# Cross-attention scores of a Perceiver block: high queries against high and low contexts in one 512-column product, the halves added together with the row maximum

## The chip, the core and the metric

One core of a Trainium2 chip runs the whole program. The metric is device time in microseconds (us) of one execution. The core has five engines that run their own in-order instruction lists and meet at semaphores: TensorE (PE; its weight loads are listed as PEld), VectorE (DVE), ScalarE (ACT), GpSimd (POOL) and SyncE (SP, which issues the transfers). Products land in PSUM, which has eight banks of 512 fp32 columns; everything else lies in SBUF.

## The reference, cut to what matters

```python
x = x + xattn(layernorm(x), ctx_768)     # the stage that is changed
x = x + attn(layernorm(x))               # relative-position attention
x = x + ffn(layernorm(x))                # fake-quantised gated FFN

# xattn: x (64, 32, 512), ctx (64, 257, 384), 16 heads of 64
q = (hidden_states @ Wq).reshape(B, S, H, Dh).transpose(0, 2, 1, 3)
k = (encoder_hidden_states @ Wk)...      # likewise
v = (encoder_hidden_states @ Wv)...
scores = jnp.einsum('bhsd,bhkd->bhsk', q, k) * scale
probs = jax.nn.softmax(scores, axis=-1)  # over the 257 context rows
out = jnp.einsum('bhsk,bhkd->bhsd', probs, v)
out = out.transpose(0, 2, 1, 3).reshape(B, S, H * Dh) @ Wo + bo
```

## The kernel before

The cross attention never forms the keys. A first stage multiplies each head's queries with that head's key weights, so that a query becomes a row of 384 numbers (`qk`) to be multiplied with the context itself. The last context row is subtracted from the other 256, which leaves the softmax as it is and makes the score of the last row zero.

To keep fp32 accuracy on a faster product, operands are held as two parts, a rounded high part and the low remainder; a product is the sum of three: high x high, high x low, low x high (`PARTS`).

Work goes by tiles of 128 tokens, 16 of them (`t`), each of four batches of 32 tokens (`b`). Tile 0 is the section "first", tile 1 "second", tiles 2 to 14 run in a loop, tile 15 is "last". In a batch, 16 heads x 32 queries make 512 score rows, in four row groups of 128 (`rg`). For one batch and row group, here called a unit, `pe_scores` (L656) multiplies `qk` (stationary, 128x128) with the transposed context `cT` (moving): three chunks of the 384 numbers, three products each, into one PSUM bank. The four units use the banks s0, s1, q0 and q1. VectorE takes the negated row maximum (`row_max`, L1200), ScalarE the exponential with its row sum straight out of PSUM (`exp`, L899), which frees the bank; VectorE inverts the sum, and ScalarE (units 0 and 1) or VectorE (units 2 and 3, `norm`) scales the row.

The written order of each engine fixes what stands behind what. TensorE's in one batch is: scores of unit 0; transposes of the probabilities of the batch before (`pe_probsT`, banks t0 and t1); scores of units 1 and 2; in the second batch the value-weight products of the heads of the tile before (`pe_wv`); scores of unit 3; first value product (`pe_pv`, banks o0 and o1 in turn, so the third one needs the bank of the first); two of three transposes of the next context (`pe_ctxT`, banks t0, t1 and t0 again, so the third one needs the bank of the first); second value product; in the fourth batch the output projection (`pe_wo`, in bank q1, the bank of unit 3's scores) with the third transpose in its middle, otherwise the third transpose; third value product.

Each transposed bank is copied by ScalarE as the high part (`act_high`, L779) and then subtracted by VectorE as the low part (`dve_low`, L976), which frees the bank. VectorE adds the last context row's share to each value product (`dve_attended`, L1182). In the fourth batch ScalarE and VectorE also split the next tile's `qk` into its parts (`act_qk_high`, `dve_qk_low`). GpSimd subtracts the last row from the contexts and splits them.

The columns for the last context row: `cT` has 258 columns, of which two are zero. In the first tile all products run over 258 columns and leave the zero score in the bank; later only the unit in bank q1 after an output projection does, the other banks keep the zero.

## Time and profile before

| | |
|---|---|
| median of 3 runs | 1561.62 us (1560.56 to 1562.24) |
| the profiled execution, its own time | 1560.53 us |
| its span, first to last instruction | 1558.7 us |
| mean granted TensorE clock | 0.997 |
| busy: TensorE, its weight loads, VectorE, ScalarE, GpSimd | 1525.8, 1281.1, 1048.9, 737.6, 381.5 us |

The span is what the views below divide; the profiled execution's own time is 1.8 us more, for what lies around it. A line such as L669 is a line of the kernel. Products are pipelined, so the duration shown for one (some 0.28 us for 256 columns) is longer than the time after which the next one starts; cadences are read from groups of many. Where a group of products waits, its weight load (PEld) waits ahead of it.

### The profile page before, as it was taken

How to read it: one execution, taken by the hardware profiler on the slowest of the kernel's cores; microseconds unless marked ns; L12 is line 12 of the kernel's file. 1: busy time of each engine (PE TensorE's matmuls, PEld its weight loads, DVE VectorE, ACT ScalarE, POOL GpSimd, SP SyncE). 2: the span in 40 equal slices, each digit the busy share in tenths (PEclk: the TensorE clock that was granted, in tenths of full speed). 3: DMA queues.
4: the chain of work that ended last, by engine and by line, in shares of the span. 5: the costliest groups of instructions: out<-in, count | busy, mean ns of one | idle time of the engine just before them, and what ended most of it. 6: DMA issues, size and time to landing. Idle time of an engine off the chain costs nothing.

```text
span 1558.7 us, 35878 instructions
## 1 busy us (share of the span) xinstructions
PE 1525.8 (98%) x13706; PEld 1281.1 (82%) x13714; DVE 1048.9 (67%) x2255; ACT 737.6 (47%) x1601; POOL 381.5 (24%) x228
## 2 busy tenths in 40 slices
PE   7999989999999999999999999999999999998989
PEld 5888788999999899989989898888888888886544
DVE  7666677677667766676677767647555654556788
ACT  5445655455545554555455554443222232234755
POOL 1000444343444344444434353500000000000000
PEclk9999999999999999999999999999999999999999
DMA  6899773341434133422343144250220311325022
GB/s 229 321 365 374 304 271 137 132 153 47 140 136 143 61 124 140 140 87 98 140 140 122 63 140 140 82 203 21 83 97 29 116 49 43 116 54 151 1 107 108
DMA packets 90270, 210.72 MB, mean 135 GB/s; under 512 B 17025, under 2 KB 45889, under 8 KB 87361
## 3 DMA queue, kind: packets, MB, share of 16 engines
q1 hardware_dynamic: 90176, 209.39, 37.7%
q8 instruction: 70, 1.15, 0.3%
q14 instruction: 24, 0.19, 0.0%
HBM read 137.54 MB, written 68.94 MB: 132 GB/s over the span
## 4 chain that ended last, share of the span: by engine, by line
PE 90%; issue 6%; DVE 3%; ACT 1%; DMA 0%; SPq 0%; POOLq 0%; POOL 0%
PE psum_o L693 17%; PE psum_s L669 9%; PE psum_q L669 8%; PE psum_o L1518 6%; PE psum_q L1562 6%; PE psum_q L723 6%; PE psum_q L1518 6%; PE psum_t L1594 6%; PE psum_o L557 6%; PE psum_o L708 5%; PE psum_t L681 3%; PE psum_t L638 3%; PE psum_t L589 1%; PE psum_q L589 1%; PE psum_s L1549 1%
## 5 line engine op out<-in xcount | busy, mean ns | idle before, releaser
L693 PE MATMUL psum_o<-pT,c_nat 128*128 128x512 f32 x1152 | 307.4, 403 | 3.4 <-issue 2.4
L693 PEld LDWEIGHTS psum_o<-pT,c_nat 128*128 128x128 f32 x1152 | 204.5, 189 | 40.2 <-DVE pT L980 3.6
L1332 POOL TENSOR_TENSOR c_nat<-c_raw,constants 128x768 fp32r<-128x768 f32 x64 | 93.8, 1466 | 551.4 <-PE psum_o L693 441.7
L1187 DVE TENSOR_SCALAR oT<-psum_o,c_last 128x512 f32<-128x512 f32 x192 | 143.4, 747 | 66.4 <-PE psum_o L693 66.3
L902 ACT ACTIVATE probs<-psum_s,nmax 128x257 f32<-128x257 f32 x128 | 61.1, 477 | 233.8 <-DVE nmax L1202 233.8
L669 PE MATMUL psum_s<-cT,qk 128*128 128x256 f32 (+1 forms) x1152 | 163.6, 286 | 1.3 <-DVE cT L980 1.2
L669 PEld LDWEIGHTS psum_s<-cT,qk 128*128 128x128 f32 x1152 | 150.0, 189 | 7.4 <-DVE cT L980 1.4
L669 PE MATMUL psum_q<-cT,qk 128*128 128x256 f32 (+1 forms) x1152 | 151.8, 283 | 0.3 <-DVE qk L1119 0.3
L669 PEld LDWEIGHTS psum_q<-cT,qk 128*128 128x128 f32 x1152 | 142.2, 189 | 3.1 <-issue 2.6
L980 DVE TENSOR_TENSOR pT<-psum_t,pT 128x512 fp32r<-128x512 f32 x128 | 87.6, 686 | 71.0 <-ACT pT L781 71.0
L1317 POOL TENSOR_TENSOR c_raw<-c_raw,last_row 128x768 f32<-128x768 f32 x64 | 120.2, 1878 | 24.2 <-DMA last_row<-in_ctx_dram 19.4
L1335 POOL TENSOR_TENSOR c_nat<-c_raw,c_nat 128x768 fp32r<-128x768 f32 x64 | 118.1, 1846 | 5.0
L2334 POOL PARTITION_ALL_REDUCE tiny<-tiny x1 | 0.4, 381 | 424.9 <-DVE tiny L2250 424.9
L781 ACT ACTIVATE cT<-psum_t 128x256 fp32r<-128x256 f32 x192 | 67.3, 388 | 76.4 <-PE psum_t L638 76.2
L1119 DVE TENSOR_TENSOR qk<-raw,qk 128x1536 fp32r<-128x1536 f32 x59 | 103.0, 1748 | 0.0
L833 ACT ACTIVATE qk<-raw 128x1536 fp32r<-128x1536 f32 x64 | 94.7, 1515 | 0.0
L708 PE MATMUL psum_o<-oT,wv 128*64 128x128 f32 x1536 | 87.4, 274 | 0.2 <-issue 0.2
L557 PE MATMUL psum_o<-xnT,wq 128*128 128x512 f32 x372 | 87.1, 392 | 0.0
L708 PEld LDWEIGHTS psum_o<-oT,wv 128*64 128x64 f32 x1536 | 83.5, 137 | 2.4 <-issue 0.4
L1562 PE MATMUL psum_q<-w2v_high,xnT 128*128 128x512 f32 x256 | 84.5, 396 | 0.0
L557 PEld LDWEIGHTS psum_o<-xnT,wq 128*128 128x128 f32 x372 | 69.2, 188 | 16.9 <-issue 2.1
L1518 PE MATMUL psum_o<-xnT,w2k_high 128*128 128x512 f32 x256 | 80.5, 395 | 0.0
(292 smaller groups left out, 3098.9 us busy)
## 6 DMA issues: line engine op xcount, KB each, us to landing
qk_by_tile<-staged SPq DMA_DIRECT2D x32, 1536.0 KB, 10.2
raw<-qk_by_tile SPq DMA_DIRECT2D x16, 3072.0 KB, 12.5
c_raw<-in_ctx_dram SPq DMA_DIRECT2D x64, 384.0 KB, 3.2
last_row<-in_ctx_dram SPq DMA_DIRECT2D x64, 192.0 KB, 4.3
out_dram<-x_out SPq DMA_DIRECT2D x32, 256.0 KB, 2.0
x_res<-in_x_dram SPq DMA_DIRECT2D x16, 256.0 KB, 2.7
x_in<-out_dram SPq DMA_DIRECT2D x4, 1024.0 KB, 7.7
x_all<-out_dram SPq DMA_DIRECT2D x1, 4096.0 KB, 13.4
```

Source lines behind the costliest of these rows:

```text
L557: m = pe.matmul(ps[:], wq[:, j, part, k, :], xnT[:, moving, k, :, :], start=(k, part, moving) == (0, 0, 0), stop=(k, part) == (KD - 1, 1))
L669: m = pe.matmul(ps[:, 0:keys], qk[:, rg, part, c, b, :], cT[b % 2][:, moving, c, 0:keys], start=(c, part, moving) == (0, 0, 0), stop=(c, p ...
L693: i = pe.matmul(ps[:], c_nat[(b - 1) % 2][:, part, k, m * P:(m + 1) * P], pT[:, moving, k, :], start=(k, part, moving) == (0, 0, 0), stop= ...
L708: i = pe.matmul(ps[64 * par:64 * par + 64, h4 * P:(h4 + 1) * P], wv[:, c, head * DH:(head + 1) * DH], oT[:, c, slot, :, :], start=c == 0, ...
L833: nc.scalar.activation(qk[:, rg, 0, :, :, :].rearrange("p c b (h q) -> p h (c b) q", h=4), raw[:, :, rg, :].rearrange("p h (a q) -> p h a ...
L1119: nc.vector.tensor_tensor(part[1], raw[:, :, rg, :].rearrange("p h (a q) -> p h a q", q=SQ), part[0].bitcast(F32), ALU.subtract).then_inc( ...
L1187: nc.vector.tensor_scalar(oT[:, m, :, (b - 1) % 4, :], ps[:].rearrange("p (s q) -> p s q", q=SQ), c_last[:, (b - 1) % 2, m:m + 1], None, A ...
L1317: nc.gpsimd.tensor_tensor(c_raw[i][:], c_raw[i][:], row_, ALU.subtract).then_inc(s_sub, 1)
L1332: G.tensor_tensor(flat(c_nat[i][:, 0, :, :]), flat(c_raw[i][:]), zero.to_broadcast([P, 2 * DC]), ALU.add).then_inc(s_chi, 1)
L1335: G.tensor_tensor(c_nat[i][:, 1, :, :], c_raw[i][:], c_nat[i][:, 0, :, :].bitcast(F32), ALU.subtract).then_inc(s_nat, 1)
L1518: m = pe.matmul(ps[:], (w2_high[w], w2_low[w])[part][:, k, j * P:(j + 1) * P], xnT2[:, moving, k, :, :], start=(k, part, moving) == (0, 0, ...
L1562: m = pe.matmul(ps[:], xnT2[:, part, k, i, :], w[moving][:, k, 512 * n:512 * (n + 1)], start=(k, part, moving) == (0, 0, 0), stop=(k, part ...
```

## The change

The two products with the high queries (against the high and the low context) become one of 512 columns, whose halves land side by side in the bank; the product of the low queries adds to the first half. So a unit is six products instead of nine, and its scores are the sum of two halves. ScalarE copies the second half from PSUM to the probability tile; VectorE adds the first half to it, writes the negated sum there and takes the running minimum of it, from 0.0 on for the last row's zero score, in one instruction; ScalarE's exponential then reads the probability tile in place. A semaphore step stands ahead of VectorE's instruction. Nothing puts the last row's zero score into the bank any more: GpSimd zeroes that column of the probability tile for each batch. The fills of `cT`'s zero columns go. ScalarE's order is rewritten: the four copies (`half`) are put in, and unit 0's exponential moves between the two probability copies.

```diff
@@ -655,19 +659,16 @@
 
         def pe_scores(pe, t, b, rg, section):
 
-            if section == "first" and rg == 0 and b < 2:
-                pe.wait_ge(s_zero, b + 1)
             if b == 0:
                 pe.wait_ge(s_qlo, 4 * t + (rg + 1))
             ps, done = empty(pe, U1(("S", b, rg), t, section))
 
-            keys = SKP if section == "first" or (b, rg) == (0, 3) else 2 * P
+            keys = 2 * P
             for c in range(KC):
                 if rg == 0:
                     wait_chunk(pe, t, b, section, c)
-                for part, moving in PARTS:
-                    m = pe.matmul(ps[:, 0:keys], qk[:, rg, part, c, b, :], cT[b % 2][:, moving, c, 0:keys],
-                                  start=(c, part, moving) == (0, 0, 0), stop=(c, part) == (KC - 1, 1))
+                m = pe.matmul(ps[:], qk[:, rg, 0, c, b, :], cT[b % 2][:, :, c, 0:keys], start=c == 0, stop=False)
+                m = pe.matmul(ps[:, 0:keys], qk[:, rg, 1, c, b, :], cT[b % 2][:, 0, c, 0:keys], start=False, stop=c == KC - 1)
             m.then_inc(done, 1)
 
         def pe_probsT(pe, t, b, section):
@@ -896,11 +897,19 @@
         def act_cross_tile(act, t, section):
             begun, more = section != "first", section != "last"
 
+            def half(b, rg):
+                ps, _ = full(act, U1(("S", b, rg), t, section))
+                nc.scalar.activation(probs[b % 2][:, rg, 0:2 * P], ps[:, 2 * P:4 * P], ACT.Copy).then_inc(s_half, 1)
+
             def exp(b, rg):
-                bk, _ = U1(("S", b, rg), t, section)
+                if rg == 0 and section == "first" and b < 2:
+                    act.wait_ge(s_zero, 2)
+                elif rg == 0:
+                    act.wait_ge(s_blank, 4 * t + (b - 1))
                 act.wait_ge(s_max, 16 * t + (4 * b + rg + 1))
-                nc.scalar.activation(probs[b % 2][:, rg, 0:SK], bank[bk][:, 0:SK], ACT.Exp, bias=nmax[:, rg:rg + 1],
-                                     accum_out=den[:, rg:rg + 1]).then_inc(drained[bk], 1)
+                both = probs[b % 2][:, rg, 0:SK]
+                nc.scalar.activation(both, both, ACT.Exp, bias=nmax[:, rg:rg + 1], scale=-1.0,
+                                     accum_out=den[:, rg:rg + 1]).then_inc(drained[U1(("S", b, rg), t, section)[0]], 1)
 
             def scale(b, rg):
                 act.wait_ge(s_rden, 16 * t + (4 * b + rg + 1))
@@ -911,30 +920,38 @@
                 act_high(act, U1(("CT", b, c), t, section), cT[(b + 1) % 2][:, 0, c, 0:2 * P], cols(2 * P))
 
             if not begun:
+                half(0, 0)
+                half(0, 1)
                 exp(0, 0)
                 exp(0, 1)
                 ctxT(0, 0)
                 ctxT(0, 1)
                 scale(0, 0)
                 ctxT(0, 2)
+                half(0, 2)
                 exp(0, 2)
                 scale(0, 1)
                 scale(0, 2)
+                half(0, 3)
                 exp(0, 3)
                 scale(0, 3)
                 act_last_scalars(act, t, 0, section)
             for b in range(0 if begun else 1, 4):
                 after = more or b < 3
-                exp(b, 0)
+                half(b, 0)
                 if late_turn(b, section):
-                    exp(b, 1)
+                    half(b, 1)
                 for k in range(2):
                     act_probsT(act, t, b, k, section)
+                    if k == 0:
+                        exp(b, 0)
+                if not late_turn(b, section):
+                    half(b, 1)
                 if b == 3 and more:
                     act_qk_high(act, t + 1, 0)
-                if not late_turn(b, section):
-                    exp(b, 1)
+                exp(b, 1)
                 scale(b, 0)
+                half(b, 2)
                 exp(b, 2)
                 scale(b, 1)
                 if b == 1 and section == "second":
@@ -945,6 +962,7 @@
                         act_wv(act, t, n, section)
                 if b == 1 and section == "second":
                     act_wo_high(act, 3)
+                half(b, 3)
                 exp(b, 3)
                 if b == 3 and more:
                     act_qk_high(act, t + 1, 1)
@@ -1155,7 +1173,6 @@
                 else:
                     for c in range(2):
                         dve_start_context(dve, c)
-                    nc.vector.memset(cT[0][:, :, :, 2 * P:SKP].bitcast(F32), 0.0).then_inc(s_zero, 1)
                 for j in range(4, 8):
                     dve_group_qk(dve, s, j)
                     if (s, j) == (GROUPS - 1, 4):
@@ -1198,8 +1215,12 @@
             begun, more = section != "first", section != "last"
 
             def row_max(b, rg):
-                ps, _ = full(dve, U1(("S", b, rg), t, section))
-                nc.vector.tensor_reduce(nmax[:, rg:rg + 1], ps[:, 0:SK], AX_X, ALU.max, negate=True).then_inc(s_max, 1)
+                bk, _ = U1(("S", b, rg), t, section)
+                dve.wait_ge(s_half, 16 * t + (4 * b + rg + 1))
+                dve.sem_inc(s_halfseen, 1)
+                both = probs[b % 2][:, rg, 0:2 * P]
+                nc.vector.tensor_tensor_reduce(both, bank[bk][:, 0:2 * P], both, -1.0, 0.0, ALU.add, ALU.min,
+                                               nmax[:, rg:rg + 1]).then_inc(s_max, 1)
 
             def inverse(b, rg):
                 taken(dve, U1(("S", b, rg), t, section))
@@ -1215,7 +1236,9 @@
                 dve_cross_low(dve, ("CT", b, c), t, section, v[:, 1, c, 0:2 * P], v[:, 0, c, 0:2 * P], 2 * P)
 
             if not begun:
-                nc.vector.memset(cT[1][:, :, :, 2 * P:SKP].bitcast(F32), 0.0).then_inc(s_zero, 1)
+                full(dve, U1(("S", 0, 0), t, section))
+                for i in range(2):
+                    nc.vector.memset(probs[i][:, :, 2 * P:SK], 0.0).then_inc(s_zero, 1)
                 row_max(0, 0)
                 row_max(0, 1)
                 inverse(0, 0)
@@ -1341,6 +1364,15 @@
             pool.wait_ge(s_xres, 16 * t)
             nc.gpsimd.tensor_tensor(x_res[:], x_res[:], bo_all[:], ALU.add).then_inc(s_xb, 1)
 
+        def pool_blank(pool, t, b, section):
+
+            if b:
+                taken(pool, U1(("S", b - 1, 3), t, section))
+            else:
+                pool.wait_ge(drained["q1"], U1.before("q1", t, section, 1))
+            pool.sem_inc(s_blankseen, 1)
+            nc.gpsimd.memset(probs[(b - 1) % 2][:, :, 2 * P:SK], 0.0).then_inc(s_blank, 1)
+
         def pool_qk_low(pool, t, rg):
 
             pool.wait_ge(s_qhi, 4 * t + (rg + 1))
@@ -1356,9 +1388,11 @@
             for rg in range(4):
                 pool_qk_low(pool, 0, rg)
             pool_split(pool, 0, 1, "first")
+            pool_blank(pool, 0, 1, "first")
             for b in range(2, 4):
                 pool_less_last(pool, 0, b)
                 pool_split(pool, 0, b, "first")
+                pool_blank(pool, 0, b, "first")
             pool_less_last(pool, 0, 4)
             full(pool, U1(("S", 3, 1), 0, "first"))
             pool.wait_ge(s_qlo, 4 + 1)
@@ -1370,10 +1404,12 @@
                     pool.wait_ge(s_qlo, 4 * t + 4)
                     pool_less_last(pool, t, b + 1)
                     pool_split(pool, t, b, section)
+                    pool_blank(pool, t, b, section)
                     continue
                 pool_split(pool, t, b, section)
                 if section != "last" or b < 3:
                     pool_less_last(pool, t, b + 1)
+                pool_blank(pool, t, b, section)
                 if b == 1:
                     pool_bias(pool, t)
             if section == "last":
```

The hunk left out declares the four semaphores `s_half`, `s_halfseen`, `s_blank` and `s_blankseen`.

## Rows read from the trace of the kernel before

**Rows 1.** The page: busy time of TensorE, share of the span, instructions.

```profile
PE 1525.8 (98%) x13706; PEld 1281.1 (82%) x13714; DVE 1048.9 (67%) x2255; ACT 737.6 (47%) x1601; POOL 381.5 (24%) x228
```

**Rows 2.** One tile by batches: stretch, length, busy of each engine, clock, DMA share, GB/s.

```profile
588.54:598.46 9.92, 9.92 (x69) 9.05 (x68) 7.47 (x20) 5.06 (x16) 5.11 (x3) 1.00 0.60 184
598.46:614.11 15.65, 15.65 (x167) 14.44 (x165) 8.05 (x20) 6.38 (x18) 6.32 (x4) 1.00 0.47 193
614.11:624.11 10.00, 10.00 (x69) 9.10 (x68) 6.74 (x18) 5.07 (x16) 5.11 (x3) 1.00 0.20 59
624.11:639.59 15.48, 15.48 (x94) 13.60 (x92) 13.27 (x22) 10.18 (x20) 5.12 (x3) 1.00 0.12 38
```

**Rows 3.** Chain of waits, same tile: start, length, what, number of instructions.

```profile
602.81 5.39 PE psum_o L708 x96
...
617.30 2.12 PE psum_q L669 x18
...
632.63 2.74 PE psum_q L723 x12
```

**Rows 4.** Timeline, third batch, TensorE and weight loads: start, length, what.

```profile
614.11 1.24 PE L669 MATMUL psum_s<-cT,qk 128*128 128x256 f32 x9
...
619.14 1.24 PEld L693 LDWEIGHTS psum_o<-pT,c_nat 128*128 128x128 f32 x6
...
622.26 0.37 PEld L638 LDWEIGHTS psum_t<-ident,c_raw 128*128 128x128 f32 x2
```

**Rows 5.** Timeline, third batch, ScalarE; in brackets idle time and its releaser.

```profile
616.32 1.08 ACT L781 ACTIVATE pT<-psum_t 128x512 fp32r<-128x512 f32 x2
618.00 0.48 ACT L902 ACTIVATE probs<-psum_s,nmax 128x257 f32<-128x257 f32 x1 [0.60 <-DVE nmax L1202]
...
619.93 0.46 ACT L902 ACTIVATE probs<-psum_q,nmax 128x257 f32<-128x257 f32 x1
620.29 0.19 ACT L902 ACTIVATION_READ_ACCUMULATOR probs<-psum_q,nmax 128x1 f32 x1
621.07 0.66 ACT L781 ACTIVATE cT<-psum_t 128x256 fp32r<-128x256 f32 x2 [0.59 <-PE psum_t L638]
```

**Rows 6.** Timeline, third batch, VectorE.

```profile
617.55 0.41 DVE L1202 TENSOR_REDUCE nmax<-psum_s 128x1 f32<-128x257 f32 x1
617.88 0.68 DVE L980 TENSOR_TENSOR pT<-psum_t,pT 128x512 fp32r<-128x512 f32 x1
618.48 0.15 DVE L1206 RECIPROCAL rden<-den 128x1 f32<-128x1 f32 x1
...
621.66 0.73 DVE L980 TENSOR_TENSOR cT<-psum_t,cT 128x256 fp32r<-128x256 f32 x2
```

**Rows 7.** Groups by line and shape: busy us, mean ns of one, idle before, releasers.

```profile
L1119 DVE TENSOR_TENSOR qk<-raw,qk 128x1536 fp32r<-128x1536 f32 x59 | 103.0, 1748 | 0.0
L833 ACT ACTIVATE qk<-raw 128x1536 fp32r<-128x1536 f32 x64 | 94.7, 1515 | 0.0
...
L980 DVE TENSOR_TENSOR cT<-psum_t,cT 128x256 fp32r<-128x256 f32 x192 | 73.8, 412 | 2.0 <-ACT cT L781 1.9
...
L781 ACT ACTIVATE cT<-psum_t 128x256 fp32r<-128x256 f32 x192 | 67.3, 388 | 76.4 <-PE psum_t L638 76.2
...
L907 ACT ACTIVATE probs<-probs,rden 128x256 f32<-128x256 f32 x130 | 66.1, 509 | 6.0 <-DVE rden L1206 1.2
...
L902 ACT ACTIVATE probs<-psum_s,nmax 128x257 f32<-128x257 f32 x128 | 61.1, 477 | 233.8 <-DVE nmax L1202 233.8
...
L1202 DVE TENSOR_REDUCE nmax<-psum_s 128x1 f32<-128x257 f32 x128 | 53.5, 418 | 16.8 <-PE psum_s L669 16.8
```

**Rows 8.** Timeline, fourth batch: first output-projection load, third context transpose's load.

```profile
632.24 0.19 PEld L723 LDWEIGHTS psum_q<-wo_high,aT_high 128*128 128x128 f32 x1
...
634.98 0.37 PEld L638 LDWEIGHTS psum_t<-ident,c_raw 128*128 128x128 f32 x2
```

**Rows 9.** Timeline, third batch, GpSimd's last instruction.

```profile
617.78 1.84 POOL L1317 TENSOR_TENSOR c_raw<-c_raw,last_row 128x768 f32<-128x768 f32 x1
```

More of the change, by code:

```diff
@@ L448, in build_kernel @@
         s_zero = sem("last_scores_zeroed")
+        s_half = sem("second_scores_copied")
+        s_halfseen = sem("second_scores_seen")
+        s_blank = sem("last_score_blanked")
+        s_blankseen = sem("exponentials_seen")
         s_chi = sem("ctx_high_ready")
```

## The prediction, made before the changed kernel ran

> **What bounds the kernel now.** I read four views, in this order. The page says that TensorE is busy for 98% of the span [rows 1]. The table by stretches, cut at the starts of the four batches of one token tile in the middle of the loop, says what a tile costs: 9.92, 15.65, 10.00 and 15.48 us, 51.05 in all. TensorE is busy in every microsecond of it at a granted clock of 1.00, while ScalarE works 51%, 41%, 51% and 66% of the time [rows 2]. So here a nanosecond taken from TensorE is a nanosecond gained, as long as nothing makes it wait. The chain of waits gives the cadences of its products: 18 of 256 columns in 2.12 us are 118 ns each, 12 of 512 columns in 2.74 us are 228 ns each [rows 3]. The timeline of the third batch, last, gives the order in which ScalarE and VectorE serve TensorE, and how long before its use each thing is ready [rows 4 to 6].
>
> **What the change takes from TensorE.** A unit (one batch, one of four row groups) has nine products of 256 columns now, 9 x 0.118 = 1.06 us. After, it has three of 512 and three of 256, 3 x (0.228 + 0.118) = 1.04 us. The number of columns stays; only three instructions' fixed part goes. That is about 0.025 us a unit, 0.10 a batch, 6 to 7 us over 256 units. If the 256-column products now wait for their weight loads (loads of 128 columns end up about as dense as the products), one behind a 512 could cost as little as 0.228 - 0.118 = 0.110: then 13 us. These are the ends of the gain; I take 0.10 a batch. The Trainium skill (TensorE: Matmul & The Clock Gate, "Back-to-back issue gap") has the gap as N/2.4 + 2.5 ns, which is 109 and 216 ns; the rows are 118 and 228, and a unit would gain 7 ns by the page, 2 us in all. Row and page differ, and I go by the row.
>
> **What it adds.** Per unit: ScalarE copies 256 columns from PSUM, 0.39 us by the same copy of the context transposes [rows 7]. VectorE's maximum (0.42 [rows 7]) gives way to one instruction that adds a PSUM and an SBUF operand, writes the sum and keeps a running minimum. No row shows it. Below it cannot be cheaper than an addition of the same shape, 0.41 [rows 7]; above it could cost the two passes that it fuses, 0.41 + 0.33 (a reduction that starts behind another instruction, from its start to the next start [rows 6]) = 0.75. It is nearest to an addition, and ScalarE's form with a sum read afterwards ends 0.09 later than the exponential alone (619.93 to 620.48 against 0.46 [rows 5]), so I take 0.41 + 0.09 = 0.50. VectorE also gets a separate semaphore step ahead of each: between nothing and 0.07, what a one-element reciprocal adds to the queue (0.15, of which 0.08 lie under the instruction ahead: 617.88 + 0.68 against 618.48 [rows 6]); I take 0.05. Exponentials read SBUF: 0.51 as the scaling does, against 0.48 [rows 7]. A hand-over between engines is 0.04 (maximum done 617.55 + 0.41 = 617.96, exponential at 618.00 [rows 5, 6]). An engine takes its next instruction some 0.1 before the last one ends (620.29 against 619.93 + 0.46 [rows 5]).
>
> The cost is not the busy time, of which both engines have room, but the order. For each unit ScalarE copies, VectorE fuses, ScalarE takes the exponential, and each queue is served in order. Behind an exponential that waits for the minimum stand ScalarE's scaling of earlier rows, the next unit's copy and, in the end, the context copies. I walk through the third batch with the trace's times of before.
>
> - Unit 0: product done 615.32 (614.11 + 1.24 = 615.35 now [rows 4]), copied 615.36 to 615.75, fused 615.84 to 616.34. The first probability copy now goes ahead of the exponential (615.80), exponential 616.38, second copy 616.88 to 617.47. It ended at 616.32 + 1.08 = 617.40 before [rows 5]. Nothing lost.
> - Unit 1: its copy stands behind that, 617.37 to 617.75; fused 617.85 to 618.35. The second probability low part on VectorE follows, 618.26 to 618.96, 0.4 later than before (617.88 + 0.68 [rows 6]). The first value product's weights load at 619.14 now [rows 4] and want to at 619.05: covered, with 0.05 left.
> - Exponential 1 at 618.38; inverse behind the low part, 618.88; scaling 619.07; copy 2 619.48 to 619.87; fused 619.96 to 620.46; exponential 620.50; scaling 621.00; copy 3 621.40 to 621.79; fused 621.88 to 622.38; exponential 3 at 622.42 with its sum read by 623.01. Before it stood at 619.93 [rows 5]: 2.5 us late.
> - Late next: the context copies on ScalarE, 622.92 (621.07 before [rows 5]), and VectorE's low part of the first, 623.35 to 623.76 (started 621.66 before [rows 6]). The third context transpose uses that bank; its weights load at 622.26 [rows 4] and would at 622.16. It can't before 623.80. TensorE stands for 1.64 us.
> - The third value product waits for VectorE's addition on its bank, done at 623.12: behind the stall, covered. The next batch's first scores too.
>
> Net of the 0.10 saved: +1.55 us. The first batch of a tile has the same order: +1.65 by the same walk. The second has 5.39 us of head products between the third and the fourth unit [rows 3], so the chain of three is over before the fourth starts: it only gains, -0.1. In the fourth batch a query copy (1.51 [rows 7]) stands between copy 1 and exponential 1, so by the same steps from 624.11 exponential 3 starts at 632.93 and its sum is read at 633.52. The output projection uses that unit's bank and loaded its first weights at 632.24 [rows 8]: it could at 632.14 and must wait until 633.56, 1.4 us. Then ScalarE's second query copy ends at 634.94; VectorE has one query low part (1.75 [rows 7]) and an addition ahead of the next, which runs from 635.28, and ends the context low part at 637.36; and the third transpose, due 634.98 - 0.10 + 1.42 = 636.30 [rows 8], waits another 1.1. Net +2.4.
>
> A tile: 1.65 - 0.1 + 1.55 + 2.4 = 5.5. Fourteen tiles are whole: 77. The first has no head or output products but the same chains in three batches, about 5; the last has no transposes in its last batch, about 4. Sum 86 us on 1560.5 of the profiled execution, which is 1.1 below the median of the runs: **1648**.
>
> Costed at nothing: GpSimd's zeroing of the last column. It stands behind a subtraction that ends at 617.78 + 1.84 = 619.62 [rows 9], and its reader is the exponential of the following batch, some 6 us later; were it not covered, every batch's first exponential would be late by what it lacks. Removed zero fills and 258-column products are too few to count.
>
> **Bounds.** Four fused instructions lie in series in the first and third batch (unit 0's by way of the second probability copy), two or three in the fourth. With 0.41 and no semaphore step: 4 x 0.14 = 0.56 less in each, 0.3 in the fourth, 4.1 a tile, 57 + 7 on 1560.5: 1625. With 0.75 and 0.07: 4 x 0.27 = 1.08 more in each and 0.8 in the fourth, 8.5 a tile, 119 + 13 on 1560.5: 1693.
>
> **The rivals.**
> - *The fused instruction costs nearly two passes*: 0.65 to 0.83. For it: two input streams, a written stream and a running value in one instruction, of which no row has a like. Against: two-input additions from PSUM run at the pace of one-input reductions (0.41 and 0.42 [rows 7]). Ten lie in series in a tile, so in 15.5 tiles each 0.1 is 15.5 us: 1671 to 1699, chance 0.22. The Trainium skill (Vector Engine (DVE) Microarchitecture Reference, "Points that are easy to get wrong") says that the shape with accumulator halves its throughput when both sources are non-bf16 in SBUF. Here one is in PSUM, so by its words it should not; no run here shows it.
> - *TensorE stays the bound*, on the other side: the chains end in time, and only the fewer instructions show: 1547 to 1555. It decides at one place: the first context low part must end by 622.12, 0.05 us after it does now. For it, ScalarE is idle half of the time. Against, 234 us of that idle time are already waits of exponentials for the row maximum [rows 7], and a queue in order adds to them. Chance 0.05.
> - *The saved and the lost cancel*, because copies overlap more than I allow: chance 0.02. Slower, but by less than 1618: 0.04.
>
> **How the numbers follow.** My forecast has 0.67, 1618 to 1670 by itself. The range 1618 to 1702 takes in the walk's bounds and the first rival; outside lie the other 0.11 and some 0.05 above. What a measurement of this kernel tells from no change is about 0.2%, 3 us. Faster 0.05, within 0.02, slower 0.93.
>
> **What would show it.** In the new trace: 118 and 228 ns in mixed order; fused instructions of about 0.5; TensorE idle ahead of the third context transpose in three batches of four, put down to VectorE's context low part, and ahead of the output projection, put down to an exponential; ScalarE waiting some 0.7 us for the minimum ahead of three exponentials of each batch; batches of 11.5, 15.6, 11.5 and 17.9 us. I would be wrong if the fused instruction ran far from 0.5, if the semaphore steps cost much more, or if TensorE, idle 1.6 us at a time, were granted a lower clock than its full stretches show [rows 2].

## The result, and the profile after

The changed kernel takes 1649.83 us (median of 4 runs, 1649.05 to 1652.97), against 1561.76 for the kernel before in the same session: a ratio of 1.0569, 95% interval 1.0551 to 1.0587. The profiled execution has a span of 1647.9 us, 89.2 more than before. Predicted were 1648, with a range of 1618 to 1702.

The page of the changed kernel, busy time and the shares of its chain of waits, answers to [rows 1]:

```profile
PE 1541.8 (94%) x12946; PEld 1238.9 (75%) x12946; DVE 1062.1 (64%) x2511; ACT 836.2 (51%) x1857; POOL 388.0 (24%) x291
...
PE 57%; issue 16%; DVE 14%; ACT 11%; DVEq 1%; ACTq 0%; DMA 0%; SPq 0%; POOLq 0%; POOL 0%
```

The shares of the chain of the kernel before:

```profile
PE 90%; issue 6%; DVE 3%; ACT 1%; DMA 0%; SPq 0%; POOLq 0%; POOL 0%
```

VectorE is hardly busier than before and ScalarE is at half of the span. No engine became the bound by its load; TensorE fell from 98% to 94%, and VectorE and ScalarE now hold a quarter of the chain instead of 4%. The share of "issue" rose too: in the cross stage it lies in the short gaps between the steps of VectorE and ScalarE. One tile by batches (first the third batch, then the fourth, first and second) answers to [rows 2]:

```profile
601.67:613.05 11.38, 10.14 (x57) 8.42 (x56) 6.91 (x22) 6.62 (x20) 5.18 (x4) 1.00 0.16 52
613.05:630.69 17.64, 15.89 (x81) 12.83 (x80) 12.95 (x27) 11.78 (x24) 5.18 (x4) 1.00 0.10 33
630.69:642.15 11.46, 10.25 (x57) 8.38 (x56) 8.04 (x24) 6.62 (x20) 5.41 (x4) 1.00 0.68 215
642.15:657.63 15.48, 15.48 (x153) 13.71 (x152) 8.48 (x25) 7.89 (x22) 6.39 (x5) 1.00 0.39 154
```

Three of four batches have a hole in TensorE's time, at a clock of 1.00; the second has none. The tile is 55.96 instead of 51.05. To compare single batches, one border in [rows 2] has to be moved: the second batch is taken there from 598.46, but its first product starts 0.10 later:

```profile
598.56 1.23 PE L669 MATMUL psum_s<-cT,qk 128*128 128x256 f32 x9
```

From that start, the first two batches of before are 10.02 and 15.55 us, not 9.92 and 15.65, and the second one became 0.07 us shorter.

The timeline of the next third batch, which begins at 657.63, is the chain itself. It stands against [rows 4 to 6] with 43.52 us taken off:

```profile
661.47 0.43 DVE L1222 CUSTOM_DVE_ANT_0 probs<-psum_s,probs 128x256 f32<-128x256 f32 x1 [0.82 <-ACT probs L902]
661.82 0.08 DVE L1222 DVE_READ_ACCUMULATOR2_ANT nmax<- 128x1 f32 x1
...
661.94 0.52 ACT L911 ACTIVATE probs<-probs,nmax 128x257 f32<-128x257 f32 x1 [0.65 <-DVE nmax L1222]
...
664.95 0.36 ACT L902 ACTIVATE probs<-psum_q 128x256 f32<-128x256 f32 x1
...
665.50 0.42 DVE L1222 CUSTOM_DVE_ANT_0 probs<-psum_q,probs 128x256 f32<-128x256 f32 x1 [1.41 <-ACT probs L902]
...
665.96 0.51 ACT L911 ACTIVATE probs<-probs,nmax 128x257 f32<-128x257 f32 x1 [0.65 <-DVE nmax L1222]
...
666.47 0.64 ACT L782 ACTIVATE cT<-psum_t 128x256 fp32r<-128x256 f32 x2
666.87 0.76 DVE L998 TENSOR_TENSOR cT<-psum_t,cT 128x256 fp32r<-128x256 f32 x2
...
667.35 0.20 PEld L642 LDWEIGHTS psum_t<-ident,c_raw 128*128 128x128 f32 x2 [1.68 <-DVE cT L998]
667.35 0.44 PE L642 MATMUL psum_t<-ident,c_raw 128*128 128x128 f32 x2 [1.24 <-DVE cT L998]
```

The same product before:

```profile
622.49 0.38 PE L638 MATMUL psum_t<-ident,c_raw 128*128 128x128 f32 x2
```

Read the chain from the bottom. TensorE's weight load waited 1.68 us for VectorE's context low part; that waited for ScalarE's context copy; that stood in ScalarE's queue behind exponential 3, and exponential 3 waited 0.65 us for the minimum, whose fused instruction had to wait for the copy. The walk had these ends at 622.42 (exponential 3), 622.92, 623.35 and 623.80; the trace, shifted, has 622.44, 622.95, 623.35 and 623.83. Only the starts of the fused instructions are some 0.10 late (665.50 is 621.98, the walk: 621.88).

The fourth batch of the tile, to be set against [rows 8] with 11.06 us added:

```profile
622.47 0.50 PE L724 MATMUL psum_q<-wo_high,aT_high 128*128 128x512 f32 x1 [0.93 <-ACT probs L911]
...
626.29 0.44 PE L642 MATMUL psum_t<-ident,c_raw 128*128 128x128 f32 x2 [0.82 <-DVE cT L998]
```

The output projection starts at 633.53 in the time of before (the walk: 633.56), the third transpose at 637.35 (the walk: about 637.4). Groups by line and shape give the new instruction:

```profile
L1222 DVE CUSTOM_DVE_ANT_0 probs<-psum_q,probs 128x256 f32<-128x256 f32 x128 | 54.4, 425 | 146.1 <-ACT probs L902 146.1
...
L1222 DVE DVE_READ_ACCUMULATOR2_ANT nmax<- 128x1 f32 x256 | 21.4, 84 | 0.0
```

Fused instruction and read-out of the minimum together end 0.43 us after the start (661.47 to 661.82 + 0.08 = 661.90 in the timeline above), not 0.50.

**Where the 89.2 us lie.** From the starts of the probability transposes: 1.9 ahead of the first, 5.3 in the first tile, 6.8 in the second, 4.92 in each of the 13 after, 2.7 in the last, 80.8 in all (the last one starts at 996.65 before and 1077.42 after). The other 8.4 come *after* the cross stage, where the change edits nothing: from that transpose to the end are 562.1 us before and 570.5 after. The chain of waits at the end of the self-attention stage of the changed kernel, and then the windows around it:

```profile
1483.69 1.08 issue
...
1496.46 3.39 issue
...
1500.74 10.75 PE psum_t L1630 x36
```

```profile
1495.00:1500.00 5.00, 1.61 (x102) 1.15 (x105) 1.73 (x4) 0.00 (x0) 0.00 (x0) 0.89 0.55 220
1500.00:1505.00 5.00, 5.00 (x50) 4.07 (x51) 1.42 (x4) 1.81 (x6) 0.00 (x0) 0.50 0.01 3
```

and the same place before:

```profile
1414.01 8.40 PE psum_t L1594 x36
```

Within the last stretch of small value products (32 columns) TensorE stood for 3.39 us for nothing that the profile names. Then the same 36 products of 512 columns took 10.75 us instead of 8.40: for the first 5 us the granted clock was 0.50, the lower of its two levels (1.2 GHz), and over all 10.75 us it was 0.77 in the mean; ahead of that TensorE had been busy 1.61 us of 5. Stall and slow products are 5.7 of the 8.4 us. Three shorter gaps of the same kind, 0.47, 1.08 and 0.27 us between 1419 and 1490, where the kernel before has none above 0.25, make 1.8 more; some 0.9 was not traced. This part was nobody's prediction, and the experiments had to find it as well.

### The profile page after: what moved, and what is told of

Its sections match the earlier page's. It is cut to its first block, busy times and chain, and to the rows that moved or that the text cites. A ratio compares the mean times of both kernels' runs of the same rounds, so it can differ in the third digit from the quotient of the medians.

```text
span 1647.9 us, 35554 instructions
## 1 busy us (share of the span) xinstructions
PE 1541.8 (94%) x12946; PEld 1238.9 (75%) x12946; DVE 1062.1 (64%) x2511; ACT 836.2 (51%) x1857; POOL 388.0 (24%) x291
## 3 DMA queue, kind: packets, MB, share of 16 engines
q8 instruction: 69, 1.13, 0.3%
## 4 chain that ended last, share of the span: by engine, by line
PE 57%; issue 16%; DVE 14%; ACT 11%; DVEq 1%; ACTq 0%; DMA 0%; SPq 0%; POOLq 0%; POOL 0%
PE psum_o L694 7%; PE psum_o L1554 5%; PE psum_t L1630 5%; PE psum_q L1598 5%; PE psum_q L1554 5%; PE psum_o L561 5%; PE psum_o L709 5%; DVE qk L1137 3%; ACT probs L902 3%; ACT probs L911 3%; PE psum_s L670 3%; ACT probs L916 2%; DVE probs L1222 2%; PE psum_t L642 2%; PE psum_q L670 1%
## 5 line engine op out<-in xcount | busy, mean ns | idle before, releaser
L911 ACT ACTIVATE probs<-probs,nmax 128x257 f32<-128x257 f32 x256 | 130.8, 511 | 120.6 <-DVE nmax L1222 119.1
L1222 DVE CUSTOM_DVE_ANT_0 probs<-psum_q,probs 128x256 f32<-128x256 f32 x128 | 54.4, 425 | 146.1 <-ACT probs L902 146.1
L670 PE MATMUL psum_s<-cT,qk 128*128 128x512 f32 x384 | 146.2, 410 | 0.2 <-DVE staged L1117 0.2
L670 PE MATMUL psum_q<-cT,qk 128*128 128x512 f32 x384 | 140.6, 401 | 0.0
L902 ACT ACTIVATE probs<-psum_s 128x256 f32<-128x256 f32 x128 | 48.3, 378 | 163.0 <-PE psum_s L671 163.0
L642 PE MATMUL psum_t<-ident,c_raw 128*128 128x128 f32 x384 | 65.8, 280 | 54.1 <-DVE cT L998 53.5
L1222 DVE CUSTOM_DVE_ANT_0 probs<-psum_s,probs 128x256 f32<-128x256 f32 x128 | 54.2, 424 | 94.7 <-ACT probs L902 94.7
L642 PEld LDWEIGHTS psum_t<-ident,c_raw 128*128 128x128 f32 x384 | 46.0, 141 | 85.8 <-DVE cT L998 74.4
L671 PE MATMUL psum_s<-cT,qk 128*128 128x256 f32 x384 | 107.9, 281 | 0.0
L671 PE MATMUL psum_q<-cT,qk 128*128 128x256 f32 x384 | 107.8, 281 | 0.0
## 6 DMA issues: line engine op xcount, KB each, us to landing
qk_by_tile<-staged SPq DMA_DIRECT2D x32, 1536.0 KB, 10.3
```

Of the source, the lines that this page charges most:

```text
L642: m = pe.transpose(ps[:, k * P:(k + 1) * P], keys[:, k, c * P:(c + 1) * P], ident[:])
L670: m = pe.matmul(ps[:], qk[:, rg, 0, c, b, :], cT[b % 2][:, :, c, 0:keys], start=c == 0, stop=False)
L671: m = pe.matmul(ps[:, 0:keys], qk[:, rg, 1, c, b, :], cT[b % 2][:, 0, c, 0:keys], start=False, stop=c == KC - 1)
L911: nc.scalar.activation(both, both, ACT.Exp, bias=nmax[:, rg:rg + 1], scale=-1.0, accum_out=den[:, rg:rg + 1]).then_inc(drained[U1(("S", b, ...
L1222: nc.vector.tensor_tensor_reduce(both, bank[bk][:, 0:2 * P], both, -1.0, 0.0, ALU.add, ALU.min, nmax[:, rg:rg + 1]).then_inc(s_max, 1)
```

## The experiments

Columns: the median of the 13 tiles in the loop ("tile"), the start of the last probability transpose ("last") and the time from there to the end ("rest"), of the profiled execution; all in us. Ratios are against the kernel before on the same chip.

| kernel | median (runs) | ratio, 95% | tile | last | rest |
|---|---|---|---|---|---|
| before | 1560.9 to 1562.1 | 1 | 51.05 | 996.65 | 562.1 |
| after | 1649.83 (4) | 1.0569 (1.0551–1.0587) | 55.97 | 1077.42 | 570.5 |
| product_alone | 1562.30 (10) | 1.0006 (0.9996–1.0016) | 50.69 | 990.04 | 570.4 |
| chain_alone | 1646.52 (4) | 1.0546 (1.0528–1.0563) | 56.10 | 1079.77 | 564.6 |
| busy_copy | 1566.42 (6) | 1.0034 (1.0021–1.0046) | 51.03 | 995.92 | 568.7 |
| copies_ahead | 1589.12 (4) | 1.0178 (1.0161–1.0195) | 52.17 | 1017.50 | 570.6 |
| step_twice | 1668.73 (4) | 1.0682 (1.0664–1.0700) | 57.06 | 1096.90 | 570.5 |
| order_rewritten | 1563.16 (10) | 1.0010 (1.0000–1.0019) | 50.69 | 992.04 | 568.4 |
| product_padded | 1566.85 (10) | 1.0029 (1.0019–1.0038) | 50.69 | 1001.24 | 564.6 |
| before_padded | 1578.88 (4) | 1.0105 (1.0088–1.0122) | 51.05 | 1007.52 | 571.2 |
| after_split | 1643.51 (4) | 1.0525 (1.0509–1.0541) | 55.98 | 1079.70 | 563.2 |
| order_split | 1556.40 (6) | 0.9971 (0.9959–0.9983) | 50.69 | 991.46 | 561.9 |
| order_split_start | 1554.87 (5) | 0.9961 (0.9947–0.9974) | 50.69 | 990.01 | 563.1 |
| product_split | 1555.38 (4) | 0.9957 (0.9940–0.9974) | 50.69 | 990.79 | 563.0 |

The theory: four instructions a unit in series, in queues served in order. The rivals: load (copies on ScalarE, fused instructions on VectorE), or the products themselves. The first four kernels take the change apart.

**product_alone: the six products without the chain.**

```diff
-                for part, moving in PARTS:
-                    m = pe.matmul(ps[:, 0:keys], qk[:, rg, part, c, b, :], cT[b % 2][:, moving, c, 0:keys],
...
+                m = pe.matmul(ps[:], qk[:, rg, 0, c, b, :], cT[b % 2][:, :, c, 0:keys], start=c == 0, stop=False)
+                m = pe.matmul(ps[:, 0:keys], qk[:, rg, 1, c, b, :], cT[b % 2][:, 0, c, 0:keys], start=False, stop=c == KC - 1)
```

> The kernel before with the six products of 512 and 256 columns alone: the maximum and the exponential read the first half of the bank as before, so the high x low half of the scores is left out. Theory of the serial chain: TensorE stays the bound and only its instructions count, 0.025 us a unit, 6 to 7 us: about 1555 us, 0.996 of before. Rival, that the wide products themselves cost (their operand in two pieces, the bank written over its full width): above 1570.

The tiles gave 0.36 us each, the cross stage ended 6.6 earlier, and the whole won nothing: the rest was 8.3 longer. The time of 1562.30 is thus neither the theory's nor the rival's. So the products are not the loss, and the late 8 us come with them, chain or no chain.

**chain_alone: nine products, with the chain.**

Against the changed kernel, next to the nine products of before:

```diff
-                nc.scalar.activation(probs[b % 2][:, rg, 0:2 * P], ps[:, 2 * P:4 * P], ACT.Copy).then_inc(s_half, 1)
+                nc.scalar.activation(probs[b % 2][:, rg, 0:2 * P], ps[:, 0:2 * P], ACT.Copy, scale=0.0).then_inc(s_half, 1)
```

> The nine products of before with the new chain: ScalarE copies the first half times zero into the probability tile, VectorE adds, ScalarE takes the exponential from there. The scores stay whole. Theory of the serial chain: the chain sets the time of three batches in four, the products only start it 0.03 us later: 1649 to 1653 us. Rival, that the products cost: nearer to 1562 than to 1650.

The chain alone carries the loss in the tiles, 56.10. The time, 1646.5, is 2.5 us under the expected range: the cross stage ended 2.4 us later than in the changed kernel, but the rest is 564.6 instead of 570.5, without the late stall.

**busy_copy: the copy's load without its place in the chain.**

```diff
...
+                nc.scalar.activation(nowhere[:], twice, ACT.Copy).then_inc(s_half, 1)
...
```

> The six products, the maximum and the exponential from PSUM as before, and ScalarE does a copy of 256 columns at each place where the changed kernel has one, after the same wait for the unit's product, but of a constant and to a place that nobody reads. The high x low half of the scores is left out. Theory of the serial chain: the extra copies cost only what they push in ScalarE's queue, at most 1 us a tile, in the fourth batch: 1555 to 1575. Rival, that it is the load on ScalarE (some 100 us more of it): above 1620.

ScalarE was busy 825.0 us, nearly the 836.2 of the changed kernel, and the tile took 51.03 us instead of 55.97. Of the 5.28 us by which the chain lengthens a tile (55.97 - 50.69), ScalarE's load explains 0.34. VectorE's is not in this kernel; order_rewritten has it.

**copies_ahead: the changed kernel, two copies moved up in ScalarE's order.**

```diff
+                half(b, 2)
                 if b == 3 and more:
                     act_qk_high(act, t + 1, 0)
                 exp(b, 1)
                 scale(b, 0)
-                half(b, 2)
+                if not (b == 1 and begun):
+                    half(b, 3)
                 exp(b, 2)
...
-                half(b, 3)
+                if b == 1 and begun:
+                    half(b, 3)
```

> The changed kernel with ScalarE's order alone rewritten: the copy of unit 2 ahead of exponential 1, that of unit 3 ahead of exponential 2 (in the second batch of a tile unit 3 stays where it is), so that no copy stands behind an exponential that waits for VectorE. Same instructions, same work. Theory of the serial chain: the first and third batch come back to 9.9 us, the fourth to 16.9, a tile to 52.4: 1590 us, 1580 to 1602. Rival, that load or the fused instruction's own cost sets the time: 1640 to 1652.

Same instructions, 61 us less. The next minimum is under way while ScalarE still takes the exponential before.

**step_twice: one more semaphore step in the chain.**

```diff
                 dve.sem_inc(s_halfseen, 1)
+                dve.sem_inc(s_halfseen, 1)
```

> The changed kernel with a second semaphore step ahead of each fused instruction. Theory (each unit's copy, step, fused instruction, exponential run one after the other in ScalarE's order, so all that lengthens the chain is paid up to five times a batch in three of four batches): a step of 0.05 to 0.07 us more adds 0.5 to 0.7 us to a tile, 8 to 11 us in all: 1657 to 1661. Rival (VectorE's or ScalarE's load, or the fused instruction's own length, not the chain): VectorE is busy 64% of the span and the step is no work, so 1650, within 2.

The sign and the place were right, the size not: +18.9 us. A step costs more than the walk had allowed. The timeline of step_twice:

```profile
658.87 0.36 ACT L902 ACTIVATE probs<-psum_q 128x256 f32<-128x256 f32 x1
659.51 0.42 DVE L1223 CUSTOM_DVE_ANT_0 probs<-psum_q,probs 128x256 f32<-128x256 f32 x1 [1.09 <-ACT probs L902]
```

From the copy's end to the fused instruction are 0.28 us, against 0.19 in the changed kernel (664.95 + 0.36 to 665.50 above): 0.09 for one step. A tile grew by 1.09, twelve times that, and it grew where the walk has the chain: from one start of the probability transposes to the next, the first batch by 0.41, the third by 0.37 and the fourth by 0.30, four, four and three steps, and the second by nothing. The changed kernel without any step was not tried.

**order_rewritten: both orders anew.** The lists (h copy, p probability part, e exponential, s and n scalings, m minimum, i inverse, a addition of the last key, c context part, q next query part, l last scalars, x output):

```diff
+        ACT_TURN = {"even": "h0 p0 p1 e0 h1 h2 e1 s0 h3 s1 e2 c0 c1 e3 l0 c2",
+                    "last": "p0 h0 p1 q0 h1 h2 e0 h3 e1 e2 e3 c0 q1 c1 l0 s0 s1 q2 c2 q3"}
+        DVE_TURN = {"even": "m0 p0 p1 m1 i0 m2 i1 m3 a0 c0 c1 i2 i3 n2 a1 n3 c2 a2",
+                    "last": "p0 m0 p1 m1 m2 m3 a0 i0 i1 q0 c0 i2 a1 i3 q1 c1 q2 n2 n3 c2 q3 a2 x0"}
```

> The changed kernel with the same instructions, and both ScalarE's and VectorE's orders of the batches written anew (copies ahead of the exponentials, in the fourth batch the scalings and the later query parts behind them; second batches and the first tile nearly as in copies_ahead). Theory (order alone made the loss): TensorE waits nowhere in the middle tiles, which take 50.7 to 51.2 us (50.69 in product_alone): 1589 less 15 times 1.0 to 1.5, so 1565 to 1575, with the stall of the late stage still in it. Rival (part of the loss is load, 128 x 0.38 us of copies on ScalarE and the fused instruction on VectorE, that no order can hide): the fourth batch stays over 16.5 us and the time over 1582.

The tile is 50.69, that of product_alone to the hundredth: copies, steps and fused instructions all fit under TensorE. The time went 2 us below the expected range: of the 25 us gained on copies_ahead in the cross stage, 4.5 are the first tile's (44.6 against 49.0, and 46.1 before), three times what was allowed for it. The copies that it hides are one a unit, 256, not the 128 of the rival.

**The late stall: product_padded and before_padded.** The page of the changed kernel counts 69 packets of the instruction queue for 1.13 MB, so 16 KB each. One of them begins some 1 us into the stall, in the stretch 1497.4 to 1497.9:

```profile
q8 instruction: 1, 0.02, 11.0%
```

The small value products ahead of the stall and behind it, with the clock as the third number from the right:

```profile
1495.36:1496.46 1.10, 1.10 (x88) 0.99 (x88) 1.00 1.07 432
1499.85:1500.74 0.89, 0.89 (x40) 0.76 (x40) 0.50 0.00 0
```

All seven kernels with this stall have it behind the 87th or 88th of these 128 products, and a packet begins 0.8 to 1.3 us after TensorE stopped. So it goes with a place in the program.

The edit, in product_alone and in the kernel before:

```diff
+            for _ in range(128):
+                pe.sem_inc(s_pad, 1)
             pe.wait_ge(s_ident, 16)
```

> Six products with the row maximum and the exponential of the kernel before (the high-by-low half is left out, as in product_alone), plus 128 semaphore increments of TensorE's queue at the start of the program, where it waits 10.6 us for its first operands. Removing three products in each unit made TensorE's program 384 instructions shorter in its static length (192 products, a weight load and a matmul each). The instruction queue fetches in packets of 16 KB, so the late part of the program sits half a packet away from where it sat. Theory (the place of the packet border decides whether TensorE runs out of instructions in the stretch of small value products): with 128 instructions put back the border lies as in the kernel before, the stall of 3.1 us and the low clock behind it are gone, and the time is 1562.3 less 6 to 7, so 1554 to 1557. Rival (the stall comes from when the stage's transfers run, or from anything else about the six products): stall and time as in product_alone, 1562.

> The kernel before, with nothing changed but 128 semaphore increments of TensorE's queue at the start of the program, under its first wait for operands. Theory (place of the 16 KB packet border in the instruction stream): the border moves to where it lay in product_alone, TensorE stands still for 3 us or more in the last stretch of small value products and the 36 products behind it run at the low clock: 1561.4 plus 5 to 7, so 1566 to 1569. Rival (something of the six products, not the place of the program): within 0.5 us of 1561.4.

Both times missed their range by some 10 us, because the increments were not hidden: TensorE's first product started at 21.7 us instead of 10.6 (product_alone) and 11.4 (before). But the rest of the program answered as the theory has it. It fell from 570.4 to 564.6 with the padding in product_alone, and rose from 562.1 to 571.2 in the kernel before, which has nine products and none of the change. The chain of waits of before_padded reads:

```profile
1425.56 3.65 issue
...
1430.10 10.34 PE psum_t L1595 x36
```

**after_split, order_split, order_split_start, product_split: the same shift at next to no cost.**

```diff
-                    m = pe.matmul(ps[:], xnT2[:, part, k, i, :], w[moving][:, k, 512 * n:512 * (n + 1)],
-                                  start=(k, part, moving) == (0, 0, 0), stop=(k, part) == (KD - 1, 1))
+                    wide = 256 if (s, n) == (2, 0) and (0, 0, 0) < (k, part, moving) < (KD - 1, 1, 0) else 512
+                    for at in range(0, 512, wide):
+                        m = pe.matmul(ps[:, at:at + wide], xnT2[:, part, k, i, :],
+                                      w[moving][:, k, 512 * n + at:512 * n + at + wide],
+                                      start=(k, part, moving) == (0, 0, 0), stop=(k, part) == (KD - 1, 1))
```

> The changed kernel with 40 products of 512 columns in the third group of the self-attention stage written as two of 256 each: the same arithmetic, and 80 more instructions in TensorE's program ahead of its last stretches of small value products, at some 0.01 us each (118 ns twice against 228 ns). Theory (where a 16 KB packet of instructions ends decides whether TensorE runs empty in a stretch of small products): the border moves out of the last stretch into the 512-column products ahead of it, the stall of 3.4 us goes and the 36 products behind it run at the high clock: 1649.8 less 6 to 7, so 1643 to 1644. Rival (in the padded kernels the stall went or came because 128 increments delayed everything by 10 us against the transfers, not by the place of the border): 1650 to 1651.

> order_rewritten with the same 40 products split. Its cross stage ended 4.6 us ahead of the kernel before, and the late stall took it back. Theory: without the stall 1563.2 less 6 to 7, so 1556 to 1557.5, ratio 0.996 to 0.9975 against the kernel before. Rival: 1563 to 1564, ratio 1.001.

> order_split with the first batch of the first tile ordered anew as well: its context transposes ahead of the second exponential on ScalarE, the last maximum ahead of an inverse on VectorE. In order_rewritten TensorE waited 0.97 us there for a context low part and 1.23 us for scaled probabilities. Theory: 0.5 to 2 us less than order_split. Rival (the first tiles are set by their loads, so what is won there is lost in the next batch, as order_rewritten's first tiles showed): within 0.5 us of order_split.

> product_alone (the high-by-low half is left out) with the same 40 products split: the prediction's first term by itself. Theory (six products a unit are worth 0.36 us a tile, and only the late stall hid it): 1562.3 less 6 to 7, so 1555 to 1556.5; order_split_start, which does the whole change, would then stand within 1.5 us of it, so that in the best order copies, steps and fused instructions cost nothing. Rival (the gain of order_split came out of its new orders, not out of the six products): 1560 or more.

All four medians came as the theory expected, and the split adds some 0.4 us ahead of the last stretch (an estimate, 40 times 0.01), not 10, which leaves little of the rival that a delay against the transfers moves the stall. Where the border of a packet lies was not read out. In the chain of waits of after_split the stall is gone, and the 36 products are as fast as before:

```profile
1497.05 8.41 PE psum_t L1633 x36
```

order_split beats both kernels, and order_split_start, with the first batch reordered too, has the lowest median: 1554.87 us, 0.39% under the kernel before. Its runs overlap with those of order_split (1555.05 to 1557.60), but the gain lies where the edit is: the first probability transpose starts at 195.30 instead of 196.76. Its tile by batches (third, fourth, first, second), with no hole left:

```profile
560.74:570.67 9.93, 9.93 (x59) 8.51 (x58) 7.05 (x22) 6.33 (x20) 5.19 (x5) 1.00 0.18 59
570.67:586.04 15.37, 15.37 (x83) 12.98 (x82) 12.61 (x26) 11.47 (x24) 5.15 (x5) 1.00 0.12 38
586.04:595.95 9.91, 9.91 (x59) 8.48 (x58) 8.16 (x25) 6.39 (x20) 5.84 (x5) 1.00 0.69 217
595.95:611.42 15.47, 15.47 (x154) 13.71 (x153) 8.26 (x24) 7.79 (x22) 6.37 (x6) 1.00 0.42 175
```

product_split, which has neither copies nor fused instructions, takes 1555.38: within the runs of each (1553.89 to 1555.66, and 1554.69 to 1555.84) the same time. The kernel before was not run with the split; it has no such stall to lose.

## Why the prediction was right, and where it was not

- *The saving of the six products*: 0.10 a batch predicted; 0.36 a tile, 0.09 a batch, measured, 6.6 us to the start of the last transposes and 6.0 in the time of product_split against before. Right, and the bound of 13 us was not approached. The formula that the prediction takes from the Trainium skill (TensorE: Matmul & The Clock Gate, "Back-to-back issue gap") is given there for a product by itself, not for a stream of weight loads and products as here, so going by the rows was right for that reason too.
- *The chain in ScalarE's order is the loss, not load*: shown by busy_copy (the load without the chain, 0.34 us a tile), chain_alone (the chain without the products, all of the loss) and order_rewritten (the same instructions in other orders, nothing of the loss in the tiles of the loop). The places were right too: the third context transpose in three batches, and the output projection. The clock did not fall in the holes: 1.00 in all four batches.
- *The fused instruction at 0.50*: it was 0.43. Both ends of the bound were fair, the value too high by 0.07. The rival of nearly two passes falls. The Trainium skill's halving rule (Vector Engine (DVE) Microarchitecture Reference, "Points that are easy to get wrong") speaks of two non-bf16 SBUF sources; with one in PSUM the trace shows 425 ns against 412 for a plain addition [rows 7], so nothing halved, and two SBUF sources no run here shows.
- *The semaphore step at 0.05*: mis-sized. Copy to fused instruction was 0.19 where the walk had 0.09 (0.04 hand-over and 0.05 step), and step_twice puts 0.09 on one more. The two errors, -0.07 and +0.10, nearly cancel in each link of the chain. That the walk's ends fit to 0.03 us is partly luck.
- *A tile +5.5*: +4.9. The batches were predicted at 11.5, 15.6, 11.5 and 17.9 and took 11.46, 15.48, 11.38 and 17.64: all a little shorter, although the waits end where the walk put them. The walk took the stall's length at the weight load, and that is where it is too long. In the kernel before, the load of the third context transpose begins at 622.26 [rows 4] and its product 0.23 later, at 622.49; after the stall, load and product begin together, at 667.35. So the load came 1.57 us later than before and the product 1.34, and the third batch grew by 1.38 where the walk has 1.55. The first batch (load 1.61 late, grown by 1.44) and the fourth (2.36 and 2.16) show the same 0.2, which is nearly all of the 0.6 a tile. To the start of the last transposes the change cost 80.8 us where 86 were forecast.
- *GpSimd's zeroing at nothing*: right; the list of waits has no wait of ScalarE for GpSimd.
- *Nothing outside the cross stage*: wrong; the forecast put it at nothing without a reason. 8.4 us lie there, and after_split, which only shifts the program, gives 7.3 of them back (570.5 to 563.2). The remaining 1.1 stays unexplained. That the median hit 1648 within 2 us is luck: this missing term more than made up for the 5 us too many in the cross stage.
- *TensorE stays the bound* (0.05) did not happen with this order, and would have with another: order_rewritten and its split forms are that rival's case. Of them order_split_start, at 1554.87, lies just within the 1547 to 1555 that it named; order_split (1556.40) and order_rewritten (1563.16, with the late stall) lie above.

## What to carry to other kernels

When a step becomes a ping-pong between two engines whose queues are served in order, lay out the order so that the next unit's first half is issued before the wait of the current one; the busy shares of both engines (51% and 64% here) will not warn you. Price the change twice, once in the order that it comes with and once in the best order: here the same work costs 5.7% or gains 0.4% (the latter with 40 products split in two against the late stall). And compare the stages that were not touched, too: removing instructions moves all later code, and what looked like "the product saves nothing" was a saving of 6 us and a stall that cost 7 elsewhere.

## What the runs showed of the hardware that was not expected

- TensorE can, it seems, run out of instructions. In a stretch of 128 small products (1.1 us for the first 88) it stood 3.1 to 3.7 us, and a 16 KB packet of the instruction queue begins within the first 1.3 us of that. The profile names no cause; that it is the supply of instructions is inferred, because the stall depends on where the program lies: 128 increments at its start removed it from product_alone and brought it into the kernel before, and 80 more instructions ahead of the stretch removed it from three kernels that had it. The Trainium skill (Advanced Engine Details and Errata, "ISA Cache") has lines of 16 KB, 256 instructions each; the packets' size agrees, and by it the 192 products that the change takes out of the program (four copies of the tile code, 48 each), with a weight load each, are an estimated 384 instructions, one line and a half. How early the next line is asked for, no run here shows.
- Each stall costs more than itself: the 36 products behind it take 10.3 to 11.1 us instead of 8.4, the first 5 us of them at a granted clock of 0.50 to 0.53.
- A semaphore step on VectorE's queue that does no work costs 0.09 us in a chain, a fifth of the fused instruction behind it.
- 128 semaphore increments at the start of TensorE's queue delayed its first product by 10 to 11 us (to 21.7), although it waited there for its operands anyway.
